# Second attention of a four-layer fp32 model: exponentials of head pairs, shared PSUM banks, keys masked on GpSimd

## What is computed

```python
def _L0_attn_b_ref(x, Wq, bq, Wk, bk, Wv, bv, Wo, bo):
    NUM_HEADS = 16
    HEAD_DIM = D_MODEL // NUM_HEADS
    ...
    q = x @ Wq + bq
    k = x @ Wk + bk
    v = x @ Wv + bv
    q = q.reshape(b, t, NUM_HEADS, HEAD_DIM)
    scores = jnp.einsum('bthd,bsd->bhts', q, k) / jnp.sqrt(jnp.float32(HEAD_DIM))
    mask = jnp.tril(jnp.ones((t, t), dtype=scores.dtype))
    scores = scores * mask - 10000000000.0 * (1.0 - mask)
    probs = jax.nn.softmax(scores, axis=-1)
    out = jnp.einsum('bhts,bsd->bthd', probs, v)
    return out.reshape(b, t, NUM_HEADS * HEAD_DIM) @ Wo + bo
x = x + _L0_attn_a_ref(_layernorm(x), ...)
x = x + _L0_ffn_ref(_layernorm(x), ...)
x = x + _L0_attn_b_ref(_layernorm(x), ...)
x = x + _L0_ffn_ref(_layernorm(x), ...)
```

## Time and profile before

| what | value |
|---|---|
| median of 3 runs | 2802.12 us (2799.71 to 2806.91) |
| profiled execution, its own time | 2800.01 us |
| span of the trace in it | 2798.3 us |
| busy: PE, DVE, ACT, POOL | 94%, 73%, 59%, 14% |
| mean granted PE clock | 0.967 |
| second attention, first projection to first matmul of the second FFN | 1828.4 to 2557.8 us |

### The profile page before, as it was taken

How to read it: one execution, slowest core, us unless ns; L and a number is a source line. 1 busy time by engine, 2 the same in 40 slices (tenths; PEclk the granted TensorE clock), 3 DMA queues, 4 the chain that set the end, 5 groups by cost and what they waited for, 6 DMA issues and landing times.

```text
span 2798.3 us, 45154 instructions
## 1 busy us (share of the span) xinstructions
PE 2620.7 (94%) x14496; PEld 2042.4 (73%) x14496; DVE 2037.5 (73%) x5225; ACT 1656.8 (59%) x3430; POOL 385.7 (14%) x813
## 2 busy tenths in 40 slices
PE   4999999999999999999999889989998989988998
PEld 3788788888888888888888667755555555545776
DVE  4677766767767777677776678878777777773887
ACT  3566666666666666665666445536666656655454
POOL 1000000000000000000110233402222212222344
PEclk8999999999999999999999989969999999998999
DMA  3665566566665666656666000000000000000000
GB/s 125 226 220 200 181 224 210 192 211 208 210 211 198 210 211 209 209 206 210 226 233 209 10 1 1 1 1 1 1 1 1 1 1 1 1 1 1 9 9 16
DMA packets 97587, 321.63 MB, mean 115 GB/s; under 512 B 11924, under 2 KB 25620, under 8 KB 97140
## 3 DMA queue, kind: packets, MB, share of 16 engines
q1 hardware_dynamic: 92650, 312.84, 32.6%
q0 software_dynamic: 1584, 4.33, 0.5%
q10 hardware_dynamic: 3120, 1.57, 0.2%
HBM read 158.53 MB, written 157.29 MB: 113 GB/s over the span
## 4 chain that ended last, share of the span: by engine, by line
PE 80%; DVE 11%; ACT 5%; issue 3%; POOL 1%; DMA 0%; SPq 0%; DVEq 0%; ACTq 0%; POOLq 0%
PE ps L243 8%; PE ps L245 7%; PE ps L244 7%; PE ps L630 7%; PE ps L743 5%; PE ps L605 5%; PE ps L604 5%; PE ps L781 5%; PE ps L643 4%; PE ps L645 4%; PE ps L644 4%; PE ps L763 4%; PE ps L675 4%; PE ps L676 4%; PE ps L677 4%
## 5 line engine op out<-in xcount | busy, mean ns | idle before, releaser
L910 ACT ACTIVATE a_Ph<-ps 128x512 fp32r<-128x512 f32 x512 | 305.9, 597 | 467.8 <-PE ps L630 467.7
L1215 DVE CUSTOM_DVE_ANT_0 a_sp<-ps,a_sp 128x1024 f32<-128x1024 f32 x256 | 313.2, 1223 | 180.0 <-PE ps L245 175.9
L980 ACT ACTIVATE r_P<-ps 128x512 f32<-128x512 f32 (+3 forms) x768 | 327.9, 491 | 187.1 <-PE ps L763 182.8
L1221 DVE TENSOR_TENSOR a_Pl<-ps,a_Ph 128x512 fp32r<-128x512 f32 x512 | 349.2, 682 | 10.0 <-ACT a_Ph L910 9.8
L604 PE MATMUL ps<-a_fa,a_ua 128*128 128x384 f32 (+2 forms) x960 | 327.2, 353 | 19.3 <-DVE a_fb L1176 13.9
L931 ACT ACTIVATE r_y<-ps 128x256 f32<-128x256 f32 x512 | 194.6, 385 | 216.6 <-PE ps L677 212.4
L903 ACT ACTIVATE a_sp<-a_sp,a_nm 128x1024 f32<-128x1024 f32 x256 | 295.0, 1152 | 32.1 <-DVE a_nm L1215 31.4
L630 PE MATMUL ps<-ident,a_sp 128*128 128x128 f32 x2048 | 309.0, 273 | 0.0
L743 PE MATMUL ps<-r_K,r_Q 128*128 128x512 f32 (+3 forms) x768 | 282.5, 403 | 18.2 <-DVE r_mx L1366 12.8
L630 PEld LDWEIGHTS ps<-ident,a_sp 128*128 128x128 f32 x2048 | 250.8, 141 | 61.7 <-issue 0.6
L605 PE MATMUL ps<-a_fb,a_ub 86*128 86x384 f32 (+2 forms) x960 | 290.8, 318 | 0.0
(11 more groups left out here) (217 smaller groups left out, 5676.0 us busy)
## 6 DMA issues: line engine op xcount, KB each, us to landing
scr<-a_rt SPq DMA_DIRECT2D x256, 576.0 KB, 3.1
a_sp<-scr SPq DMA_DIRECT2D x256, 512.0 KB, 4.4
a_wc<-wsp SPq DMA_DIRECT2D x24, 512.0 KB, 5.5
wsp<-a_wc SPq DMA_DIRECT2D x8, 512.0 KB, 5.6
a_ub<-a_ua SPq DMA_DIRECT2D x64, 44.0 KB
a_w1st<-in_w1t POOLq DMA_DIRECT2D x8, 256.0 KB, 4.6
out<-x SPq DMA_DIRECT2D x4, 512.0 KB, 3.2
a_w1r<-in_w1r POOLq DMA_DIRECT2D x8, 254.0 KB, 4.4
```

The source lines that it names most:

```text
L910: e.activation(self.Ph[:, n % 3, :], ps[:, 4 + n % 2, :], ACT.Copy).then_inc(S["p_hi"], 1)
L980: e.activation(self.P[:, pt, off:512], ps[:, bank, off:512], ACT.Exp).then_inc(S["b_exp"], 1)
L1215: e.tensor_tensor_reduce(out=w, in0=ps[:, 2:4, :].rearrange("p a n -> p (a n)"), in1=w, scale=-1.0, scalar=3e38, op0=ALU.add, op1=ALU.min, ...
L1221: e.tensor_tensor(self.Pl[:, n % 3, :], ps[:, 4 + n % 2, :], self.Ph[:, n % 3, :].bitcast(F32), ALU.subtract).then_inc(S["p_lo"], 1)
```

## The change

In the second attention only. Scores are made for two heads (q = 0, 2 and q = 1, 3) in two neighbouring banks, 2 and 3 or 4 and 5, and one ACT instruction takes the exponential of both; `P` has 4 buffers of two heads. PE's order in a block is both pairs, then `b_pv` of the block before. Bank 2 goes from the maxima to the scores; banks 0, 1 and 7 rotate for maxima and all small uses together. The projection's second pass on ACT is gone: ACT writes the low part's source `yh` straight from the bank with a masked bias and scale, and DVE finishes from the same bank, which is held until then; the plan puts `b_in2` right before the bank's next use. The query scale moves into the weights. `K` is written by POOL, four full-height multiplications by a row mask for each half, instead of ACT copies; its zeroing is gone. POOL masks both heads of a pair in one instruction. The maxima come in the order of the pairs.

```diff
-NP = 7
+NP = 4
+KV = 4
...
-        return [("b_in", b, 4, 0), ("b_in", b, 4, 1), ("b_in2", b, 4, 0), ("b_in2", b, 4, 1)] + keys[0] + [
-            ("b_in", b, 0, 0), ("b_in", b, 0, 1), ("b_in2", b, 0, 0), ("b_in2", b, 0, 1)] + keys[1] + [("b_vals", b)]
+        return [("b_in", b, g, half) for g in (4, 0) for half in range(2)] + [("b_vals", b)]
...
-        m = [("b_max", b, g, I, q, part) for I in range(7, -1, -1) for q in range(4) for part in range(1 + I // 4)]
-        q = [(u, b, g + 1, half) for u in ("b_in", "b_in2") for half in range(2)] if g < 3 else first(b + 1) if b + 1 < B else []
+        m = [("b_max", b, g, I, q, part) for I in range(7, -1, -1) for part in range(1 + I // 4) for q in (0, 2, 1, 3)]
+        q = [("b_in", b, g + 1, half) for half in range(2)] if g < 3 else first(b + 1) if b + 1 < B else []
...
-                r += [("b_s", b, g, ch, J, q) for q in range(3)] + prev + [("b_s", b, g, ch, J, 3)]
-                price += [0.75 * w + 54] * 3 + [1.67 * pw] * len(prev[:1]) + [300] * len(prev[1:]) + [0.75 * w + 54]
+                r += [("b_s", b, g, ch, J, 0), ("b_s", b, g, ch, J, 1)] + prev
+                price += [1.6 * w + 80] * 2 + [1.67 * pw] * len(prev[:1]) + [300] * len(prev[1:])
...
+    ring, at, held, done = (0, 1, 7), 0, {}, []
+    for u in out:
+        shares = u[0] in ("b_in", "b_vals", "b_max", "b_shift2", "b_norm2", "b_out", "b_out2")
+        bank = ring[at % 3] if shares else 7 if u[0] in ("ln_turn", "gt_logits") else None
+        while bank in held or held and u[0] == "b_max" and [v for v in held.values() if v[2] in (u[2], 4)]:
+            done.append(held.pop(next(iter(held))))
+        done.append(u + (bank,) if shares else u)
+        at += shares
+        if u[0] == "b_in":
+            held[bank] = ("b_in2",) + u[1:] + (bank,)
+    return done
...
+                if u[0] == "b_in2":
...
+                    if g == 4:
...
+                        e.wait_ge(S["b_y2"], nin)
+                        for v in range(KV):
+                            e.tensor_scalar(self.K[:, b % 2, v, os], self.Kf[:, half, :],
+                                            self.lowmask[:, 2 + v:3 + v], None, ALU.mult).then_inc(S["b_keys"], 1)
...
-                        e.affine_select(out=self.P[:, pt, off:off + 128], in_=self.P[:, pt, off:off + 128],
+                        e.affine_select(out=self.P[:, slot, :, off:off + 128], in_=self.P[:, slot, :, off:off + 128],
...
-                free[7] = S["b_y"], nin
+                free[bank] = S["b_y2"], nin
...
                 if I == 7 and q == 0 and part == 0:
                     e.wait_ge(S["b_y2"], 10 * b + 4 + 2 * g)
-                    if g == 0:
-                        e.wait_ge(S["b_keys"], 8 * b + 8)
+                    e.wait_ge(S["b_keys"], 2 * KV * (b + 1))
...
+                for k in range(2):
+                    bank, q = 2 + 2 * pr + k, pr + 2 * k
+                    rows = slice(32 * (q - q % KV), 32 * (q - q % KV + KV))
+                    e.wait_ge(*free[bank])
+                    i = e.matmul(ps[:, bank, off:512], self.K[rows, b % 2, q % KV, 128 * J:128 * J + 128],
+                                 self.Q[rows, b % 2, g, 512 * ch + off:512 * ch + 512], start=True, stop=True)
+                    free[bank] = S["b_exp"], nst
...
-                e.activation(self.y[:, k, :], ps[:, 7, :], ACT.Identity, bias=self.bq[:, g:g + 1],
-                             scale=DB ** -0.5 if g < 4 else 1.0).then_inc(S["b_y"], 1)
...
-                e.activation(self.yh[:, k, :], self.y[:, k, :], ACT.Copy).then_inc(S["b_yh"], 1)
-            elif u[0] == "b_keys":
...
-                e.activation(self.K[32 * q:32 * q + 32, b % 2, q, os], self.yk[32 * q:32 * q + 32, half, :],
-                             ACT.Copy).then_inc(S["b_keys"], 1)
...
+                e.activation(self.yh[:, k, :], ps[:, bank, :], ACT.Identity, bias=self.bl[:, g:g + 1],
+                             scale=self.lowmask[:, m:m + 1]).then_inc(S["b_yh"], 1)
...
-                e.activation(self.P[:, pt, off:512], ps[:, bank, off:512], ACT.Exp).then_inc(S["b_exp"], 1)
+                e.activation(self.P[:, slot, :, off:512], ps[:, bank:bank + 2, off:512], ACT.Exp).then_inc(S["b_exp"], 1)
...
-                e.scalar_tensor_tensor(dst, self.yh[:, k, :].bitcast(F32), self.lowmask[:, m:m + 1], self.y[:, k, :],
-                                       ALU.mult, ALU.add).then_inc(S["b_y2"], 1)
+                e.scalar_tensor_tensor(dst, ps[:, bank, :], self.bq[:, g:g + 1], self.yh[:, k, :].bitcast(F32),
+                                       ALU.add, ALU.subtract).then_inc(S["b_y2"], 1)
```

More of the change, by code:

```diff
@@ L172, in first @@
     def first(b):
-        keys = [[("b_keys", b, half, q) for q in range(4)] for half in range(2)]
-        return [("b_in", b, 4, 0), ("b_in", b, 4, 1), ("b_in2", b, 4, 0), ("b_in2", b, 4, 1)] + keys[0] + [
-            ("b_in", b, 0, 0), ("b_in", b, 0, 1), ("b_in2", b, 0, 0), ("b_in2", b, 0, 1)] + keys[1] + [("b_vals", b)]
+        return [("b_in", b, g, half) for g in (4, 0) for half in range(2)] + [("b_vals", b)]
     def prepare(n):
@@ L233, in plan_b @@
             done += price[i]
-            while i >= 4 and side and spent * total < goal * done:
-                h = side.pop(0)
-                out.append(h)
-                spent += cost(h)
+            while i >= 2 and side and spent * total < goal * done:
+                for h in side[:2] if [v[0] for v in side[:2]] == ["b_max"] * 2 else side[:1]:
+                    out.append(side.pop(0))
+                    spent += cost(h)
         out += side
-    return out + tail + late
+    out += tail + late
+    ring, at, held, done = (0, 1, 7), 0, {}, []
[9 more added lines that the diff above has]
+    return done
 def mm3(e, out, lh, ll, rh, rl):
@@ L713, in tensor_attention_b @@
             if u[0] == "b_in":
-                _, b, g, half = u
+                _, b, g, half, bank = u
                 cs = slice(L * b + 512 * half, L * b + 512 * half + 512)
@@ L742, in tensor_attention_b @@
                 e.wait_ge(*free[bank])
[L743 to L744 removed]
+                rows = slice(32 * (q - q % KV), 32 * (q - q % KV + KV))
+                e.matmul(ps[:, bank, 0:w], self.Q[rows, b % 2, g, 128 * I:128 * I + 128],
+                         self.K[rows, b % 2, q % KV, 512 * part:512 * part + w], start=True, stop=True).then_inc(S["b_mmm"], 1)
```

213 lines of the change are left out of this document (106 added, 107 removed).

## The result

The changed kernel takes 2827.53 us (median of 4 runs, 2825.43 to 2828.37) where the kernel before takes 2803.3 on the same chip: ratio 1.0085, 95% interval 1.0068 to 1.0103. It is 24 us slower (19 to 29); I had forecast 31 us faster, and the time lies above my range.

What follows compares the result with a forecast made beforehand. Neither DVE (32.0 us a group) nor PE (33.4) fills 42.2 us; three fixed-order queues wait for each other. Terms -49 + 17 + 6 + 0 - 3 - 2 = -31 give 2771 us, range 2730 to 2812.

Steps and rivals of the forecast that it cites:

- Terms (1) to (3): In order: exponentials in pairs; one projection pass fewer (18 us); key copies off ACT (15.0); ACT loses 55 to 94 us.
- Rival F: Pair exponentials on ACT pay their fixed cost twice: 2787 us; chance 0.08 together with milder returns up to 2793.
- (4): Groups 0 to 14: four score banks instead of three return half of DVE's 98.6 us of waits, -49 us.
- (5): Shared ring of three banks: each of 34 `b_in` costs DVE a 0.5 us refill, +17 us; bounds 0 and +55.
- (6): Key multiplications on POOL stand before the masks of diagonal blocks: +6 us; bounds 0 and +38.
- (9): Opening: key halves on POOL take 5.4 to 6.4 us each; DVE starts about 2 us earlier or at the same time, -2.
- (8): Group 15: rounds of four heads take 2.1 us instead of 2.62, six rounds, -3 us; bounds 0 and -5.
- A: Groups 0 to 14: the waiting loop dissolves further, a group takes 38.5 us instead of 42.2; 2741 us, chance 0.15.
- D: Keys on POOL hold the masks in full, 32 to 38 us instead of 6; about 2800 to 2804 us, chance 0.05.
- E: POOL and DVE hinder each other during 24 key multiplications, 33 to 38 us more; about 2806 us, chance 0.02.
- C: The ring decides: about 109 small uses each cost DVE a 0.5 us refill; slower, 2833 to the median, chance 0.13.

Runs made afterwards that it cites:

- e6: Changed kernel with the projection through ACT's `y` again, so its bank is free after ACT and not after `b_in2`; 2818.47 us, 1.0055 of the kernel before.
- e13: e10 with the short projection and its bank held until `b_in2` put back; 2794.61 us, 0.9971 of the kernel before.
- e5: Changed kernel with the keys copied by ACT again; 2819.56 us, 1.0065 of the kernel before.
- e14: e10 with the keys on POOL put back; 2786.93 us, 0.9944 of the kernel before.
- e16: e10 without pairs: one head per exponential, score banks 3, 4 and 5; 2815.31 us, 1.0043 of the kernel before.
- e10: The fast variant: changed kernel with LayerNorm turns and gate logits in rotation, old maxima order, keys on ACT, projection through `y`, old maxima/projection prices, single maxima; 2779.11 us.
- e3: Changed kernel without pairs: one head per exponential over banks 2 to 5, old prices of the scores; 2847.76 us, 1.0162 of the kernel before.
- e1: Kernel before with maxima and small uses rotating together over banks 0, 1 and 7, nothing held; 2804.42 us, 1.0011 of the kernel before.
- e4: Changed kernel with LayerNorm turns and gate logits taken into the rotation instead of always writing bank 7; 2816.92 us, 1.0048 of the kernel before.
- e17: e10 with LayerNorm turns and gate logits back on bank 7 out of turn; 2789.19 us, 0.9958 of the kernel before.
- e18: e10 with maxima taken from the side list two at a time, at the old prices; 2792.05 us, 0.9968 of the kernel before.
- e15: e10 with the new order of the maxima put back; 2790.03 us, 0.9947 of the kernel before.
- e2: Changed kernel with the old banks (maxima 0 to 2, single-head scores 3 to 5, small uses 7); 2855.61 us, 1.0188 of the kernel before.

## Why the prediction was wrong

**Terms (1) to (3), right in price, worthless in part.** ACT lost 60 us where I had 55 to 94. A pair of 512 took 1024 ns, and a run of two 1.94 us, so a pair starts 0.92 after the one before it: exactly the value of the overlapped case. Rival F (the pair pays its fixed cost twice) is refuted by 1024 against 2 x 599. By the Trainium skill, ScalarE: Activation LUTs, section "What ACT_TABLE_LOAD costs", the pair would be 186 + 0.833 x 1024 = 1039 ns, an estimate; the trace agrees within 2%. But e6 and e13 show that the second pass wasn't worth taking from ACT at the price of a held bank, and e5 and e14 point the same way for the key copies, with 5 us of each seen in the opening. I had let (2) and (3) count toward the return of (4) because they shortened ACT, without asking at whose expense.

**Term (4), the mechanism right, the size too large.** I expected PE's waits for ACT under 50 us, and 14 were left. The premise was misread: the 110.1 us count 26.1 twice, since the matmuls' waits of the earlier trace rows lie inside the weight loads' 52.4. PE waited 84.0 us for ACT, less than the 100.0 for DVE, and had no matmul for only 50.2 us in all. I took half of DVE's 98.6 us for what returns, -49, which is nearly all of PE's idle time. Four score banks and pairs give 36 us where nothing else stands in the way (e16), about 29 of them in groups 0 to 14 and 5 in group 15, and 98.6 falls to 81.0 (e10). In the changed kernel pairs are worth 21 (e3). So this term was too large by some 20 us even in its best setting.

**Terms (5) and (6), and what had no term: the step that failed.** I had charged 17 for the ring and 6 for the keys, 23 in all, and called everything else free without a reason from a row. Undoing the held bank, the keys, the turns on bank 7, the order, the twos and the prices together gives 48 us (e10 against the changed kernel); one by one in the fast variant they come to 69, with the large uncertainty said above.
- The ring (5). I priced each `b_in` as a refill of DVE, 0.5 us. In e1 a turn in the ring costs nothing that can be told; what costs is that the bank waits for DVE's `b_in2`, which stands in DVE's queue behind the maxima, while PE's next maximum stands before the bank. The wait is 34.5 / 22 = 1.6 us at PE, up to 3.0, not 0.5. 8 to 16 us in the time happens to be my 17, so the sum wasn't wrong there, but the reason was. It also settles the trade: held bank against 0.54 us of ACT, and the bank was dearer.
- LayerNorm turns and gate logits, 10 to 12 us. The diff showed them, on `7` as ever, and I read "as ever" as "free". But 7 is now one of three rotating banks. A turn on it comes out of order, so it needs a bank that DVE may still be reading, and the maxima that then fall to bank 7 wait for it (9.9 us above). That this is how the time is lost is only argued: with the turns in the rotation most of those waits stay (8.6 in e4; 6.7 in e17 against 6.4 in e10).
- Order of the maxima and prices of the plan. I read them as bookkeeping: order 6 to 9, twos 15, prices 9, all 0 in my sum. DVE's waits for maxima don't carry them: in groups 0 to 14 they are 81.0 us in e10, 79.8 in e17, 76.7 in e18 and 81.5 in e15. PE's idle time does: against e10 it grows by 9.1 us with the twos, 6.2 with the order and 4.3 with the turns on bank 7, and the stretch by 9.0, 6.2 and 4.1. With the twos it is the idle time behind DVE's maxima that grows, by 11.2 us: PE stands in front of a bank that DVE has not freed. For the order and the turns it is spread over several causes, and why is open.
- The keys (6). The forecast was 6 for the masks held in mid layer, and the changed kernel shows about that: PE is idle 7.6 us for masks (2.29 of them above), 2.7 in e5. The measured 6 to 8 us mostly lie elsewhere: in the opening, term (9).

**Term (9).** I let the first maximum come 2 us earlier or at the same time. From the first projection it comes at 16.7 us against 17.2, so 0.5 earlier. I compared only with the kernel before; without keys on POOL the other edits would have brought it to 11.4 (e5), and this gain was eaten before it could be seen. POOL's eight in a row started at 1833.7, 3.3 us after the first projection, and ended at 1846.1, and PE stood 8.12 us before them. Then the maxima of group 0 took 41.0 us instead of 36.6, with a granted clock of 0.54 instead of 0.62 and DVE busy 2.0 us longer; I had 0 for that, and e5 shows that it isn't due to the keys.

**Term (8), right.** Rounds of four heads in group 15, ACT's timeline:

```profile
2561.77 1.94 ACT L992 ACTIVATE r_P<-ps 128x1024 f32<-128x1024 f32 x2 [0.19 <-PE ps L789]
2564.13 1.94 ACT L992 ACTIVATE r_P<-ps 128x1024 f32<-128x1024 f32 x2 [0.43 <-PE ps L789]
2566.24 1.94 ACT L992 ACTIVATE r_P<-ps 128x1024 f32<-128x1024 f32 x2 [0.17 <-PE ps L789]
2568.61 1.02 ACT L992 ACTIVATE r_P<-ps 128x1024 f32<-128x1024 f32 x1 [0.43 <-PE ps L789]
```

They start (2568.61 - 2561.77) / 3 = 2.28 us apart, against 2.62 in the earlier trace rows and 2.1 forecast; the group is 4.4 shorter, where I had 3 and at most 5. This is where the change works as meant: there are no maxima, so no held bank and no interleaving.

**The rivals.** A needed the loop to dissolve further; even the fast variant doesn't reach 2741. D and E are out: the masks lost 4.9 us and not 32, and DVE's reductions take 2.48 us for four beside POOL's multiplications (at 2156.79) and 2.48 with POOL idle (at 1847.07). But E's "no row shows a DVE instruction lengthened beside POOL" holds only for the rows picked. The kernel before has three such places, DVE's `b_in2` and a mask of POOL:

```profile
2194.20 0.81 DVE L1342 SCALAR_TENSOR_TENSOR r_Q<-r_yh,lowmask,r_y 128x512 fp32r<-128x512 f32 x1
...
2194.53 0.64 POOL L507 TENSOR_SCALAR_AFFINE_SELECT r_P<-r_P 128x128 f32<-128x128 f32 x1
```

Alone they take 0.75 and 0.31, and the mask ends some 0.2 us after DVE's instruction. It reads two SBUF tensors; the changed kernel's L1358, a bank and one SBUF tensor, takes at most 0.75 us in 25 executions beside POOL. That agrees with the Trainium skill, SBUF - State Buffer, section "SBUF: two separate sides", by which a GpSimd instruction and a DVE one with two SBUF inputs exclude each other. The cost here is a few tenths of a us each time. C came nearest in time, 2833 against 2827.5, and its sign was there: DVE's waits for maxima above 98.6, PE's new waits behind `b_in`. But its mechanism, each of some 109 small uses costing DVE a refill, isn't borne out: e1 has all of them in the ring for at most 7 us, and e10 has them too and DVE's waits at 81.0, below 98.6. Held uses cost, out-of-turn ones do once ACT no longer sets the pace, and in the right column 41 of the 69 us aren't in the ring at all. My own test named the outcome: PE's waits for ACT fell and DVE's share of 76% did not rise. It gave this too little weight: in a loop where PE waits longer for DVE (100.0 us) than for ACT (84.0), each new coupling between PE and DVE takes from the same idle time that relief of ACT is to give back.

**Still open.** Why e2 loses 53 us: that is about what its parts come to in the right column (16 + 8 + 9 + 24 = 57) and far more than in the left (8 + 6 + 6 + 2 = 22). How the order, the prices and the turns on bank 7 act. Whether small uses in the ring cost something beside pairs. An earlier `b_in2` in the changed kernel, with the short projection kept, wasn't tried. The granted clock in groups 0 to 14 was 0.95 after and 0.97 before, for 6.7 us more of PE's busy time; whether that is part of the loss or its consequence no run here separates.

## What to carry to other kernels

When engines walk one list in fixed order, price an edit by who waits for whom after it, not by whose work it shortens: a buffer in a rotation is cheap as long as its first reader frees it, and dear when it waits for a later unit of another queue. Read every line of a diff that changes the list, its order and its prices as a change of its own; here twos and prices cost 24 us in the best setting, against 36 that the pairs gained. Try the parts of a bundle in both directions, out of the whole and into the best rest, since one loss can hide another: twos and prices looked like 2 us from one side and like 24 from the other. And do not add the waits of weight loads and of matmuls: they are mostly the same stalls.
